# A decoder block on one core: six stages with starts of their own, and stacked rows by DMA from SBUF

## What is computed

```python
# recurrent attention; bit_linear rounds rows to 8 bits and weights to -1, 0, 1
h = rms_norm(x, g_pre)
a = sigmoid(bit_linear(h, w_a) + decay_bias)
i_gate, v = sigmoid(bit_linear(h, w_i)), bit_linear(h, w_v)
rec_out = chunked_scan(a, sqrt(clip(1.0 - a * a, 1e-08)) * (i_gate * v))
ffn_out = bit_linear(silu(bit_linear(rms_norm(rec_out, g_post), w_gate)), w_down)
x = layernorm(x + rec_out + ffn_out)
# cross-attention, 16 heads of 16
Q, K, V = heads(x @ Wq.T + bq), heads(ctx @ Wk.T + bk), heads(ctx @ Wv.T + bv)
scores = rope(Q) @ rope(K).T * SCALE            # masked
x = layernorm(x + softmax(scores) @ V @ Wo.T + bo)
# three layers with weights +1 and -1: 512 -> 1024 -> 1024 -> 256, and a layernorm
```

## Time and profile before

| | us |
|---|---|
| median of 3 runs (lowest to highest) | 890.74 (890.59 to 890.93) |
| the profiled execution | 888.45 |
| its span | 886.7 |
| PE busy | 800.9 (90%) |
| DVE busy | 642.4 (72%) |
| ACT busy | 549.2 (62%) |
| POOL busy | 296.9 (33%) |

### The profile page before, as it was taken

The page is one execution under the profiler, slowest core; times in us unless marked ns, Lnnn a source line. Parts: engine busy times, 40 slices in busy tenths (PEclk is TensorE's granted clock), DMA queues, the critical chain, the costliest instruction groups (busy, mean ns, idle before and its releaser), DMA issues.

```text
span 886.7 us, 17907 instructions
## 1 busy us (share of the span) xinstructions
PE 800.9 (90%) x6856; PEld 626.3 (71%) x6890; DVE 642.4 (72%) x1224; ACT 549.2 (62%) x917; POOL 296.9 (33%) x476
## 2 busy tenths in 40 slices
PE   1687899999999999999999999999999999998986
PEld 1444477877877787877878777877777787876665
DVE  6658486886959596886959595977869595966442
ACT  4644857657494847667584848567584948573432
POOL 7753314152333324151433324151423334141001
PEclk9999999999999999999999999999999999999999
DMA  9033332415042332316042433415061423223000
GB/s 298 13 66 66 67 67 51 71 31 115 14 105 41 79 66 56 78 32 114 14 109 36 80 66 56 84 42 98 14 125 21 89 44 63 59 50 72 1 13 25
DMA packets 52517, 57.47 MB, mean 65 GB/s; under 512 B 7856, under 2 KB 48848, under 8 KB 49360
## 3 DMA queue, kind: packets, MB, share of 16 engines
q1 hardware_dynamic: 52432, 56.31, 30.0%
HBM read 39.24 MB, written 16.79 MB: 63 GB/s over the span
## 4 chain that ended last, share of the span: by engine, by line
PE 61%; DVE 16%; ACT 9%; DMA 4%; issue 4%; POOL 3%; SPq 1%; DVEq 0%; ACTq 0%; POOLq 0%
PE bankC L1118 18%; PE bankA L1053 6%; PE bankC L1102 6%; PE bankA L987 6%; PE slotB L1021 6%; PE slotB L1040 5%; PE bankA L922 5%; DMA q_st<-m_lo 4%; DVE u L1304 2%; ACT pr L794 2%; PE bankA L903 2%; DVE bn L1359 2%; ACT sqT L682 2%; ACT L794 2%; POOL rstd L574 2%
## 5 line engine op out<-in xcount | busy, mean ns | idle before, releaser
L1118 PE MATMUL bankC<-h0h,w 128*128 128x256 f16 x1024 | 233.7, 273 | 0.6 <-DVE h0l L1452 0.5
L1118 PE MATMUL bankC<-h0l,w 128*128 128x256 f16 x1024 | 233.3, 272 | 0.0
L1408 DVE TENSOR_REDUCE nmax<-slotB 128x4 f32<-128x1024 f32 x128 | 150.7, 1216 | 1.8 <-PE slotB L1021 0.3
L794 ACT ACTIVATE pr<-slotB 128x1024 f32<-128x1024 f32 x128 | 127.5, 1028 | 13.3 <-PE slotB L1040 13.0
L1118 PEld LDWEIGHTS bankC<-h0h,w 128*128 128x128 f16 x1024 | 99.9, 98 | 15.2 <-issue 1.2
L1118 PEld LDWEIGHTS bankC<-h0l,w 128*128 128x128 f16 x1024 | 100.1, 98 | 14.2
L1040 PE MATMUL slotB<-q_st,k_st 99*128 99x256 bf16 x512 | 74.7, 274 | 13.4 <-DMA q_st<-m_lo 11.2
L573 POOL TENSOR_SCALAR rstd<-mv 128x2 f32<-128x2 f32 x48 | 9.3, 193 | 215.6 <-DVE mv L1362 214.5
L1021 PE MATMUL slotB<-k_st,q_st 97*128 97x256 bf16 x512 | 76.7, 272 | 4.2 <-DVE nmax L1408 2.5
L1040 PEld LDWEIGHTS slotB<-q_st,k_st 99*128 99x128 bf16 x512 | 43.9, 97 | 38.3 <-DMA q_st<-m_lo 15.9
L1102 PE MATMUL bankC<-xh,w 128*128 128x256 f16 x256 | 57.8, 273 | 14.3 <-DVE xl L1446 13.7
(11 more groups left out here) (206 smaller groups left out, 1752.0 us busy)
## 6 DMA issues: line engine op xcount, KB each, us to landing
k_st<-scr SPq DMA_DIRECT2D x96, 128.0 KB, 4.5
q_st<-scr SPq DMA_DIRECT2D x96, 128.0 KB, 4.3
scr<-kpart SPq DMA_DIRECT2D x16, 384.0 KB, 2.8
scr<-qpart SPq DMA_DIRECT2D x16, 384.0 KB, 2.7
x<-in_x SPq DMA_DIRECT2D x16, 256.0 KB, 3.7
cT<-in_ctxT SPq DMA_DIRECT2D x16, 256.0 KB, 2.7
out<-x SPq DMA_DIRECT2D x16, 256.0 KB, 2.2
pr<-in_k SPq DMA_DIRECT2D x1, 1024.0 KB, 9.6
```

The lines of the kernel that those rows point to most:

```text
L794: act.activation(pr[i % 2][:, c, :, :].rearrange("p h s -> p (h s)"), slotB[ringB.slot(g, name)][:, :], ACT.Exp, scale=DH ** -0.5).then_in ...
L1118: ins = pe.matmul(bankC[ringC.slot(g, name)][:, e * T:(e + 1) * T], w_1[:, i // 2, (2 * m + e) * P:(2 * m + e + 1) * P], (h0h, h0l)[i % 2] ...
L1408: dve.tensor_reduce(nmax[:, hg * HG * NT + n:(hg + 1) * HG * NT:NT], slotB[ringB.slot(g, name)][:, :].rearrange("p (h s) -> p h s", s=S), ...
```

## The change

- `TIMES` becomes a dictionary of seven tables: "weights" and six stages (recurrent, keys, queries, scores, values, network). `BEGIN` gives each stage its own start for each group: 47.296 apart in the middle, at other distances in the first and last groups. All planned times are new. `when(step, engine, g)` adds the two, for `order` and `Ring` alike.
- By the new tables the exponentials of a group come after the next group's keys, values and queries have been started, and their second half lies between the score steps of the next group; every later step (oTok to store) is one group deeper behind the recurrent steps than before, and kT follows q.
- `put`, `kput`, `qput` and the DRAM buffer scr are gone. `stack` copies from the part tile in SBUF straight into the stack: for each of the six places two DMAs (one per chunk c) of 8 partitions x 16 runs of 512 B, 64 KB each. The DMAs of part i are issued once part i is made (kh_s, kp1_s, kparts; qh_s, qp1_s, qparts), in the order 0, 1, 2. For this `q_parts` counts its second part on a semaphore, qp1_s.
- The writers of kpart and qpart (`first_part`, `k_parts`, `kparts_`, `q_parts`) wait for the arrival of the previous group's stack instead of for its way to DRAM.

```diff
-BEGIN = [0, 53.194, 106.603, 159.927, 213.209, 266.528, 319.858, 373.172, 426.486, 479.8, 533.114, 586.428, 639.742, 693.116, 746.368, 799.574]
+BEGIN = {
...
+    "queries": [0, 47.545, 107.13, 154.245, 201.541, 248.837, 296.132, 343.428,
+                390.724, 438.02, 485.315, 532.611, 579.907, 627.256, 674.621, 729.917],
+    "scores": [0, 58.27, 108.251, 155.525, 202.82, 250.116, 297.412, 344.708,
+               392.003, 439.299, 486.595, 533.891, 581.186, 628.273, 675.917, 730.068],
+    "values": [0, 50.39, 97.808, 144.955, 192.25, 239.546, 286.842, 334.138,
+               381.433, 428.729, 476.025, 523.321, 570.616, 618.229, 666.766, 715.64],
...
+def when(step, engine, g):
+    return BEGINS[step][g] + AT[step][engine]
...
-    steps = [(BEGIN[g] + at[engine], n, step, g)
-             for n, (step, at) in enumerate(AT.items()) if engine in at
-             for g in range(1 if step.startswith("w:") else G)]
+    steps = [(when(step, engine, g), n, step, g)
+             for n, (step, at) in enumerate(AT.items()) if engine in at for g in range(len(BEGINS[step]))]
...
-            def put(g, n, parts, made, gone):
-
-                if g >= 2:
-                    sp.wait_ge(*(kst_in, qst_in)[n].at(g - 2))
+            def stack(g, dst, parts, i, which, made, arrived):
+
                 sp.wait_ge(*made.at(g))
-                sp.dma_start(scr[g % 2, n].rearrange("i (c p) t -> p (i c) t", p=P),
-                             parts[:, :, :, :].rearrange("p i c t -> p (i c) t")).then_inc(gone.sem, 16)
...
-            def stack(g, dst, n, which, arrived):
-                for s, i in enumerate(which):
-                    sp.dma_start(dst[DH * s:DH * (s + 1), :, :],
-                                 scr[g % 2, n, i].rearrange("(d h) t -> d h t", d=DH)).then_inc(arrived.sem, 16)
+                for s, part in enumerate(which):
+                    if part == i:
+                        for c in range(CT):
+                            r = DH * s + DH // CT * c
+                            sp.dma_start(dst[r:r + DH // CT, :, :], parts[:, i, c, :]).then_inc(arrived.sem, 16)
...
-                stack(g, k_st[g % 2], 0, PARTS_K, kst_in)
+                stack(g, k_st[g % 2], kpart, 0, PARTS_K, kh_s, kst_in)
+                stack(g, k_st[g % 2], kpart, 1, PARTS_K, kp1_s, kst_in)
+                stack(g, k_st[g % 2], kpart, 2, PARTS_K, kparts, kst_in)
...
-                sp.wait_ge(*qout.at(g))
-                stack(g, q_st[g % 2], 1, PARTS_Q, qst_in)
+                stack(g, q_st[g % 2], qpart, 0, PARTS_Q, qh_s, qst_in)
+                stack(g, q_st[g % 2], qpart, 1, PARTS_Q, qp1_s, qst_in)
+                stack(g, q_st[g % 2], qpart, 2, PARTS_Q, qparts, qst_in)
...
             def q_parts(g):
                 if g >= 1:
-                    dve.wait_ge(*qout.at(g - 1))
+                    dve.wait_ge(*qst_in.at(g - 1))
                 dve.wait_ge(*qh_s.at(g))
                 own.settle(dve.tensor_tensor(qrest[:, :, :], qt1[:, :, :], qpart[:, 0], ALU.subtract))
-                own.settle(dve.tensor_scalar(qpart[:, 1], qrest[:, :, :], 1.0, None, ALU.mult))
+                dve.tensor_scalar(qpart[:, 1], qrest[:, :, :], 1.0, None, ALU.mult).then_inc(qp1_s.sem, 1)
+                dve.wait_ge(*qp1_s.at(g))
```

More of the change, by code:

```diff
@@ L89 @@
 ENGINES = ("PE", "ACT", "DVE", "POOL", "SP")
 def times():
[L93 to L98, removed]
-AT = times()
+    table, begin = {}, {}
+    for stage, text in TIMES.items():
+        for entry in text.replace("\n", "|").split("|"):
+            if entry.strip():
+                step, *at = entry.split()
+                table[step] = {ENGINES["PAVGS".index(t[0])]: float(t[1:]) for t in at}
+                begin[step] = BEGIN[stage]
@@ L131, in __init__ @@
         until, n = [0.0] * len(full), [0] * len(full)
-        for start, name, g in sorted((BEGIN[g] + AT[name]["PE"], name, g) for name in items for g in range(G)):
+        for start, name, g in sorted((when(name, "PE", g), name, g) for name in items for g in range(G)):
             engine, last = items[name]
@@ L135, in __init__ @@
             self.where[(name, g)] = (s, n[s])
-            until[s] = BEGIN[g] + AT[last][engine]
+            until[s] = when(last, engine, g)
             n[s] += 1
@@ L470, in later @@
                 return lambda g: load(g + 2) if g + 2 < G else None
-            steps = {"w:mask": mask_row, "loadx": later(loadx), "loadc": later(loadc), "kput": kput, "kget": kget,
-                     "qput": qput, "qget": qget, "maxrow": maxrow, "store": store}
+            steps = {"w:mask": mask_row, "loadx": later(loadx), "loadc": later(loadc), "kget": kget,
+                     "qget": qget, "maxrow": maxrow, "store": store}
             for step, g in order("SP"):
@@ L836, in _ @@
                      "w:rope": angles, "w:bqk": qk_bias, "kT": keys, "v": values, "q": queries,
-                     "kp": lambda g: first_part(g, kt_s, kt1, kpart, kout, kh_s), "x1T": x1T_,
-                     "qp": lambda g: first_part(g, qr_s, qt1, qpart, qout, qh_s), "max": max_high,
+                     "kp": lambda g: first_part(g, kt_s, kt1, kpart, kst_in, kh_s), "x1T": x1T_,
+                     "qp": lambda g: first_part(g, qr_s, qt1, qpart, qst_in, qh_s), "max": max_high,
                      "pv1": lambda g: weighted(g, 0), "pv3": lambda g: weighted(g, 2), "oT": oT_, "x2T": x2_high,
@@ L1382, in k_parts @@
                     dve.wait_ge(*kparts.at(g - 1))
+                    dve.wait_ge(*kst_in.at(g - 1))
                 dve.wait_ge(*kh_s.at(g))
```

98 lines of the change are left out of this document (56 added, 42 removed).

## The result

The changed kernel takes 1,040.17 us (median of 4 runs, 1,031.41 to 1,054.64) against 890.66 for the kernel before, a ratio of 1.1645 with a 95% interval of 1.1567 to 1.1723. The forecast was 1,010 in a range of 866 to 1,045. The ratio leaves out the slowest of the four runs, which is over 1.5% above the fastest. The runs differ from each other by 2%, where those of the kernel before differ by 0.05%. The profiled execution took 1,037.79.

A forecast was written before the change was run, and what follows sets the result against it. PE (TensorE), busy 90%, was taken as the bound, with a new stack wait of about 9.7 us a period deciding the sum: 147 + 688 + 137 + 34 gives a span of 1,006, forecast 1,010 us, range 866 to 1,045.

The forecast's parts named there:

- a wait for k's rows ahead of score0: On PE each period: rows all in 32.1 us after q's start against 22.4 of work, so about 9.7 of wait.
- The price of a DMA: One 64 KB stack DMA into 8 partitions: 0.96 us taken, from a rate of 8 GB/s per partition.
- The low bound, 0.44: Lowest time for one 64 KB stack DMA, 0.44 to 0.50 us, from issue cost or 131 GB/s kept.
- rival B: Stack copies hidden at 0.44 to 0.50 us a DMA, no wait: 869 span, about 873 us; chance 0.29.
- first x2T: Start of the span: 140 plus 7 for two stacks waited for, 147 us.
- twelve intervals: Middle periods of 57.3 us each (46.2 work, 9.7 stack wait, 1.4 other gaps): 688 us.
- the last three: Last intervals between x2Ts, without recurrent or query work of a later group: 121 plus 16 for two score waits, 137 us.
- 47.8 if nothing new waits: PE's period in the new order: 46.2 us of work plus 1.6 of gaps, without stack waits.
- 139 to 140 without any stack wait: Longer start of the deeper order, from 118 to 139 to 140 us, stack waits left out.
- Rival E: DVE's maxima and the exponentials, sharing two slots of slotB, hold PE 1 us a period: 885 to 895; chance 0.04.
- D: Stack DMAs into 8 neighbours reach 2 ports: 1.2 us a DMA, near 1,095 us; chance 0.05.
- C: Stack DMAs in between, 0.55 to 0.8 us each: 895 to 955 us; chance 0.06.

The follow-up runs named there:

- experiment 1: Changed kernel with the stacks' rows spread, each 64 KB DMA writing 8 partitions 6 apart instead of 8 neighbours: 937.67 us, ratio 1.0512 to the kernel before.
- experiment 2: Changed kernel with each 64 KB stack DMA filling half the columns of 16 neighbouring partitions instead of all columns of 8; scores not real: 951.38 us (one run).
- Experiment 6: Changed kernel with 52 useless 512-column matmuls on PE ahead of score0's wait, from the third group on: 1,041.63 us, ratio 1.1660 to the kernel before.
- Experiment 9: Changed kernel with rows spread 6 partitions apart and POOL issuing six of k's stack DMAs, SP the rest: 864.66 us, ratio 0.9701 to the kernel before.
- experiment 3: New order of all steps with the old way of stacking, through DRAM and 128 KB DMAs into 16 partitions: 1,003.78 us, ratio 1.1254 to the kernel before.
- experiment 11: Changed kernel with neighbouring rows kept, but stack DMA issue shared by SP and POOL: 1,009.10 us, ratio 1.1305 to the kernel before.
- experiment 12: Changed kernel with stack's two loops exchanged (all places for chunk 0, then chunk 1), rows neighbouring: 1,055.79 us, ratio 1.1856 to the kernel before.
- experiment 5: Changed kernel with k's twelve stack DMAs and mask row issued by POOL, q's staying on SP, rows neighbouring: 1,044.05 us (one run).
- experiment 10: Changed kernel with rows spread 6 apart and ten of k's twelve stack DMAs left out from the third group on: 865.06 us, ratio 0.9701 to the kernel before.
- experiment 4: Old order of all steps with the new stacks straight from SBUF, 64 KB DMAs into 8 neighbouring partitions: 914.98 us, ratio 1.0265 to the kernel before.

## Why the prediction was right

The range, 866 to 1,045, held a gain as well as a loss, and the time lies only 5 below its upper end. What was right is the direction, the mechanism and four fifths of the loss (119 of 150).

**The bound.** The forecast's mechanism, a wait for k's rows ahead of score0, is what the profile shows: 9.6 a group against 9.7 forecast, PE's work ahead of it 22.9 against 22.4. That the mean agrees to 0.1 is luck in part: hardly a group waits 9.7, and the forecast's one price for a DMA stands between two measured ones.

**The price of a DMA** came out at 1.03 where the copying is slow (0.96 forecast) and at 0.67 in the groups where it isn't, and the reason given was only half right. It was read from the rate per partition (8 GB/s); experiments 1 and 2 show that eight partitions take 98 GB/s if they are spread, and that sixteen take the same 64 KB at the issue's rate. Nor is one DMA into 8 neighbours slow by itself: the first of a group went at 119 GB/s. The narrow thing is the neighbourhood once DMAs follow each other closely; why, and why not in every group, no run shows. The low bound, 0.44, was wrong as well: it was the issue cost of a DMA with 16 long runs, and one with 128 short runs takes SP 0.67. With that, rival B in its own form (stacks hidden behind one queue) was impossible: 24 x 0.67 + 9.8 is 25.9, more than 22.9. Its chance of 0.29 was too high.

**The ports.** The Trainium skill's rule, "SBUF — State Buffer", section "Door 1: The DMA port swizzle", has the direction that experiment 1 shows: neighbours reach few ports, spread rows many (by its map 6 to 8 for these rows; the expectation's 7 holds for some of them). Its size doesn't hold here: by it 8 neighbours would take 54 GB/s at most (an estimate from its figure for a port), and the first DMA of a group went at 119, the window at 576 shows 97, and even the slow copying 62 to 64. The other page that was drawn on, "DMA: Bandwidth & Descriptors", section "Why small descriptors are slow (HBM only)", has short runs within SBUF free of the price of short runs; experiment 2 agrees for the transfer (84 GB/s at the pace of the issue), while their issue costs 0.67 instead of 0.44.

**The sum, term by term** (the x2T ahead of an xh copy is 0.7 earlier):

| | forecast | measured |
|---|---|---|
| first x2T | 147 | 154.9 |
| twelve intervals | 688 | 702.5 |
| the last three | 137 | 144.9 |
| after the last x2T | 34 | 33.0 |
| span | 1,006 | 1,035.3 |

The step that was off is in the first section: "the granted clock is 1.00 (2.4 GHz) throughout, so the clock is no term here". That holds for the kernel before, but the forecast itself put a pause of 9.7 us into each period, and after one PE starts at 1.2 GHz. Experiment 6 prices it at 1.3 to 2.2 a period.

Experiment 9 lets the sum be parted. The forecast has 866 without any stack wait and 139 of waits (7 + 12 x 9.7 + 16). Measured are 864.8, the span of experiment 9 (4.5 of such waits are still in it), and 142.1 of waits ahead of the score matmuls in the changed kernel (124.3 for k's rows, 5.3 for q's, and 12.5 in two groups whose releaser the profile doesn't name). Both terms are right to 3 us. What is left of the 1,035.3 is 28.4, the size of the whole difference, and the forecast had nothing for it. The same reckoning leaves 26 to 32 in experiments 1, 2, 3, 11 and 12, whose waits are 3 to 11 us a group (38 in experiment 5). So this term goes with the number of the waits and hardly with their length, about 2.2 for each of the 13, as the half clock seen behind them would. That the clock is all of it isn't shown.

**The order.** "47.8 if nothing new waits": 47.0 to 47.3 a group in experiments 9 and 10. The start, "139 to 140 without any stack wait", is 140.6 (141.3 less 0.7). Rival B's 869 for the span is 864.8. So the working of what the order wins was right, and so was the forecast that it would not be won. One comparison in it misleads: for the last three intervals of the kernel before it took 3 x 49.1 = 147, the mean over all fifteen, where they measure 139.8; the sum doesn't use it. Rival E, waits of the maxima and exponentials in their two shared buffers, falls with experiments 9 and 10; D's 1,095 wasn't reached, and C is where experiments 1 and 2 came to lie, by their issue (by C's scale 0.67 a DMA is 915) and the slow clock. Table loads of the exponential: 28, forecast 31; they lie beside PE's work, as forecast:

```profile
L815 ACT ACT_TABLE_LOAD x28 | 35.9, 1283 | 3.0 <-PE slotB L1061 0.9
```

**What the part on the change missed** is the order's share in the loss. The text weighed the new DMAs; experiment 3 shows that with the old ones the new order still takes 1,003.8. Against the 890.7 before, the new DMAs alone cost 24 (experiment 4), the new order alone 113 (experiment 3), both together 150. The larger part is owed to k's and q's copying standing side by side, which the text named, but priced for the new DMAs only.

## What to carry to other kernels

A copy that was hidden is a budget: when an order moves two of them next to each other, add up issue and transfer of both against the work that is left between, for the old way of copying and for the new. Rows that a queue of DMAs writes within SBUF were better laid out with a stride than side by side here, and once that was done the many small DMAs cost their issuing queue most. And once a forecast puts a pause of some us on TensorE, the slow clock behind it is a term of the sum, here about 2.2 a pause.

## What the hardware showed that I had not expected

- One kind of DMA has two rates in one kernel: 64 KB into 8 neighbouring partitions went at 97 GB/s (share 0.59) in one group and at 64 GB/s (share 0.66) in another; with the partitions 6 apart it went at its issue, 98 GB/s (share 0.36). The first DMA of the slow group was quick too, 119 GB/s, and 2 us later the rate was 62. What tips a group from one to the other isn't shown.
- After a pause of 3.9 us (experiment 1) PE restarted at a granted clock of 0.50, as it did after the 12.4 of the changed kernel.
- SP took 0.67 us for the issue of a DMA with 128 runs of 512 B, and 0.44 for one with 16 runs of 8 KB in the kernel before (0.49 and 0.52 for such ones in experiment 3).
